# Neighbourhood attention and MLP on one core: K's window copies move from GpSimd to ScalarE, two instruction lists are reordered, and the GELU is evaluated twice

## What is computed

```python
def _na2d(x, qkv_w, qkv_b, proj_w, proj_b, num_heads=8, k=3):
    qkv = x @ qkv_w + qkv_b
    q, kk, v = jnp.split(qkv, 3, axis=-1)          # q is scaled by hd ** -0.5
    nb_k = kk[:, ri, ci]                           # the 3 x 3 neighbours of each point
    nb_v = v[:, ri, ci]
    attn = softmax(einsum('bijnd,bijmnd->bijnm', q, nb_k))
    return einsum('bijnm,bijmnd->bijnd', attn, nb_v) @ proj_w + proj_b
h1 = n1_w * arcsinh(h) + n1_b
h = h + _na2d(h1, qkv_w, qkv_b, proj_w, proj_b)
h2 = n2_w * arcsinh(h) + n2_b
out = h + gelu(h2 @ mlp_w1 + mlp_b1, approximate=False) @ mlp_w2 + mlp_b2
```

## Time and profile before

| | |
|---|---|
| device time, median of 3 runs | 4930.54 us (4923.46 to 4935.97) |
| the profiled execution | 4926.99 us, its span 4925.2 us |
| busy share of the span | PE 90%, POOL 82%, DVE 76%, ACT 68% |
| granted TensorE clock, mean | 0.979 |

### The profile page before, as it was taken

One profiled execution on the slowest core, in us unless ns is written; L12 is line 12 of the kernel. 1 busy time (PEld: TensorE's weight loads), 2 busy tenths in 40 slices (PEclk: granted clock), 3 DMA queues, 4 the chain that ended last, 5 costly groups with the idle time before them and its releaser, 6 DMA issues.

```text
span 4925.2 us, 149526 instructions
## 1 busy us (share of the span) xinstructions
PE 4412.7 (90%) x53320; PEld 3254.9 (66%) x53320; DVE 3742.0 (76%) x7717; ACT 3338.3 (68%) x4865; POOL 4059.1 (82%) x5498
## 2 busy tenths in 40 slices
PE   3899999999999999999999999999999999999997
PEld 2666666666666666667666666666676666666665
DVE  4777777777778777778777777777787777787774
ACT  2676667666667666767766676666676666776774
POOL 1788888888888888888888888888888888888885
PEclk8999999999999999999999999999999999999999
DMA  3555555555555555555555555555555555555552
GB/s 79 130 129 124 126 127 128 127 129 123 125 129 131 125 125 131 126 127 133 126 123 126 127 129 127 127 124 125 128 130 125 124 128 124 129 131 125 127 125 59
DMA packets 1330837, 610.98 MB, mean 124 GB/s; under 512 B 862990, under 2 KB 1326992, under 8 KB 1327632
## 3 DMA queue, kind: packets, MB, share of 16 engines
q1 hardware_dynamic: 1330192, 601.81, 51.7%
HBM read 208.17 MB, written 135.40 MB: 70 GB/s over the span
## 4 chain that ended last, share of the span: by engine, by line
POOL 47%; issue 32%; PE 16%; ACT 3%; POOLq 1%; DVE 1%; SPq 0%; ACTq 0%; DMA 0%; DVEq 0%
PE ps L387 15%; POOL p_lo L1058 9%; POOL b_lo L1077 8%; POOL g_lo L1087 7%; POOL g_hi L1085 6%; POOL k_win L1105 5%; POOL gate L1052 5%; POOL b_hi L1075 3%; POOL k_win L1115 2%; ACT p_hi L994 1%; POOL k_win L1124 1%; ACT L1003 1%; ACT prob L993 0%; POOLq L1055 0%; POOL a_lo L1067 0%
## 5 line engine op out<-in xcount | busy, mean ns | idle before, releaser
L1058 POOL TENSOR_TENSOR p_lo<-prob,p_hi 100x512 f16<-100x512 f32 x1024 | 1341.8, 1325 | 283.4 <-ACT p_hi L994 283.4
L993 ACT ACTIVATE prob<-ps 100x512 f32<-100x512 f32 x1024 | 614.0, 600 | 968.5 <-PE ps L387 967.4
L821 DVE TENSOR_REDUCE ps<-ps 128x8 f32<-128x800 f32 x512 | 511.0, 998 | 380.2 <-PE ps L387 377.2
L1052 POOL TENSOR_TENSOR gate<-gate_in 1x1 f32<-1x1 f32 x894 | 301.5, 337 | 488.1 <-DVE ln_u L747 434.0
L852 DVE TENSOR_TENSOR o_norm<-ps,recip 64x128 f32<-64x128 f32 x2048 | 591.3, 289 | 52.1
L1087 POOL TENSOR_TENSOR g_lo<-g,g_hi 128x512 f16<-128x512 f32 x512 | 593.2, 1159 | 40.9
L994 ACT ACTIVATE p_hi<-ps 100x512 f16<-100x512 f32 x1024 | 615.4, 601 | 0.0
L387 PEld LDWEIGHTS ps<-v_win,p_hi 100*128 100x128 f16 x8192 | 484.0, 98 | 180.1 <-issue 14.3
L387 PE MATMUL ps<-w_hi,g_hi 128*128 128x256 f16 x2048 | 559.4, 273 | 0.0
L387 PE MATMUL ps<-w_lo,g_hi 128*128 128x256 f16 x2048 | 559.4, 273 | 0.0
L387 PE MATMUL ps<-w_hi,g_lo 128*128 128x256 f16 x2048 | 559.3, 273 | 0.0
(11 more groups left out here) (105 smaller groups left out, 12676.4 us busy)
## 6 DMA issues: line engine op xcount, KB each, us to landing
keys<-k_win SPq DMA_DIRECT2D x1536, 100.0 KB, 2.2
v_win<-v_rows SPq DMA_DIRECT2D x1024, 101.6 KB
queries<-q_nat SPq DMA_DIRECT2D x1536, 64.0 KB
v_rows<-v_nat SPq DMA_DIRECT2D x256, 260.0 KB, 4.4
xin<-in_x_dram SPq DMA_DIRECT2D x128, 512.0 KB, 4.0
out_dram<-y SPq DMA_DIRECT2D x256, 256.0 KB, 2.7
queries<-in_query_mask_dram SPq DMA_DIRECT2D x128, 240.0 KB
keys<-in_mlp_w_dram SPq DMA_DIRECT2D x2, 512.0 KB, 6.7
```

The source lines that it names most:

```text
L821: v.tensor_reduce(maxima_of_pair(), ps[:, B_S:B_S + 2, 0:PAIRS * NK].rearrange("p n (a k) -> p n a k", k=NK), AX.X, ALU.max).then_inc(max3 ...
L993: act.activation(prob[b][0:NK], ps[0:NK, B_ST + b, :], ACT.Exp, scale=INV * INV).then_inc(prob_ready, 1)
L1052: pool.tensor_tensor(gate[:, n:n + 1], gate_in[:], gate_in[:], ALU.add)
L1058: pool.tensor_tensor(p_lo[b][0:NK], prob[b][0:NK], p_hi[b][0:NK], ALU.subtract).then_inc(p_lo_ready, 1)
```

## The change

K's window copies become ScalarE instructions: the 4 copies of 640 numbers stay four, the 8 copies of 80 become 2 of 320. They stand in slot 0 (bottom rows and high parts) and at the end of slot 2 (low parts and top rows). The GELU is evaluated twice on ScalarE, to fp32 and to fp16, and GpSimd's four casts go. Five of GpSimd's seven `pass_waits` go with the groups that they stood in. On ScalarE the second `q_high` moves next to the first, and `log1_` moves from behind the two tiles of slot 3 to ahead of them. On VectorE the second `q_low` moves up to the first, `sign1` moves up ahead of tile 6's normalisation, and `magnitude1` and `magnitude2` move down.

```diff
@@ VectorE, step
-                    if k == 1 and post:
-                        magnitude2(t - 1, old)
                     if k == 1 and pre:
                         q_low(t + 2, par, 0)
-                    if k == 2 and fill:
-                        magnitude1(t + 3, (u + 3) % XT)
+                        q_low(t + 2, par, 1)
+                    if k == 1 and fill:
+                        x_from_transposes(t + 3, (u + 3) % XT, 0)
...
+                    if k == 3 and fill:
+                        sign1(t + 3, (u + 3) % XT)
 
                     if att:
                         sum_reciprocal(t, 2 * k)
...
                     if k == 1 and post:
+                        magnitude2(t - 1, old)
                         sum2_(t - 1)
...
+                    if k == 2 and fill:
+                        magnitude1(t + 3, (u + 3) % XT)
                     if k == 2 and fin:
                         result(t - 2, 0)
@@ ScalarE
+            def windows_main(t, par, lo):
+
+                act.wait_ge(k_lo_ready, signals(t, G, G))
+                act.wait_ge(k_in[par], landed(t - 2, K_DMAS))
+                for g in range(G):
+                    a = k_nat[:, lo, g]
+                    rows = bass.AP(a.tensor, a.offset, [list(a.ap[0]), [TS, TILES], [PITCH, TS], [1, WIN]])
+                    to = k_win[par][:, lo, g].rearrange("p c (r j) -> p c r j", j=WIN)
+                    s = act.activation(to[:, :, 1:1 + TS], rows, ACT.Copy)
...
+            def windows_top(t, par):
+
+                act.wait_ge(k_in[par], landed(t - 2, K_DMAS))
+                window_edge(par, 0, TS - 1).then_inc(win_top, 1)
...
-                    act.activation(g32[:, m, :], ps[:, IN_BANK[m], :], ACT.Gelu, bias=b1[:, m:m + 1],
+                    act.activation(g32[:, m, :], ps[:, IN_BANK[m], :], ACT.Gelu, bias=b1[:, m:m + 1], scale=INV)
+                    act.activation(g_hi[:, m, :], ps[:, IN_BANK[m], :], ACT.Gelu, bias=b1[:, m:m + 1],
                                    scale=INV).then_inc(gelu_ready, 1)
@@ ScalarE, step
+                    if k == 3 and fill:
+                        log1_(t + 3)
                     if att:
                         probabilities(t, 2 * k)
@@ GpSimd
-                    pool.tensor_copy(g_hi[:, m, :], g32[:, m, :]).then_inc(g_hi_ready, 1)
-                    pool.wait_ge(g_hi_ready, signals(t, MT, m + 1))
```

More of the change, by code:

```diff
@@ L142, in build @@
         b2 = sb("b2", [P, C], F32)
-        gate_in, gate = sb("gate_in", [1, 1], F32), sb("gate", [1, 7], F32)
+        gate_in, gate = sb("gate_in", [1, 1], F32), sb("gate", [1, 2], F32)
         xin = sb("xin", [P, BLOCKS, C], F32)
@@ L215, in build @@
             sem("act_" + s) for s in ("q_hi", "k_hi", "v_hi", "o_hi", "gelu", "prob", "p_hi"))
-        a_hi_ready, a_lo_ready, b_hi_ready, b_lo_ready, g_hi_ready, g_lo_ready, p_lo_ready = (
-            sem("pool_" + s) for s in ("a_hi", "a_lo", "b_hi", "b_lo", "g_hi", "g_lo", "p_lo"))
-        win_main, win_bottom, win_top = (sem("pool_win_" + s) for s in ("main", "bottom", "top"))
+        a_hi_ready, a_lo_ready, b_hi_ready, b_lo_ready, g_lo_ready, p_lo_ready = (
+            sem("pool_" + s) for s in ("a_hi", "a_lo", "b_hi", "b_lo", "g_lo", "p_lo"))
+        win_main, win_bottom, win_top = (sem("act_win_" + s) for s in ("main", "bottom", "top"))
         block = ctx.enter_context(nc.Block())
@@ L892, in step @@
                         h_from_projection(t - 1, old, (u - 1) % XT, 1)
-                    if k == 1 and pre:
-                        q_low(t + 2, par, 1)
                     if k == 1 and fill:
-                        x_from_transposes(t + 3, (u + 3) % XT, 0)
                         x_from_transposes(t + 3, (u + 3) % XT, 1)
                     if k == 1 and post:
+                        magnitude2(t - 1, old)
                         sum2_(t - 1)
@@ L907, in step @@
                         result(t - 2, 1)
-                    if k == 3 and fill:
-                        sign1(t + 3, (u + 3) % XT)
                     if att:
@@ L972, in k_high, with window_edge, windows_bottom @@
                                ACT.Identity, bias=bqk[:, G + g:G + g + 1]).then_inc(k_hi_ready, 1)
+            def windows_main(t, par, lo):
[6 more added lines that the diff above has]
+                    s = act.activation(to[:, :, 1:1 + TS], rows, ACT.Copy)
+                if lo == 1:
+                    s.then_inc(win_main, 1)
+            def window_edge(par, at, row):
+                a = k_nat[:, 0, 0]
+                rows = bass.AP(a.tensor, a.offset + row * PITCH,
+                               [list(a.ap[0]), [TS * PITCH, 2 * G], [TS, TILES], [1, WIN]])
+                to = k_win[par][:].rearrange("p l g c (r j) -> p (l g) c r j", j=WIN)
+                return act.activation(to[:, :, :, at], rows, ACT.Copy)
+            def windows_bottom(t, par):
+                act.wait_ge(k_lo_ready, signals(t + 1, G, G))
+                window_edge(par, WIN - 1, 0).then_inc(win_bottom, 1)
+            def windows_top(t, par):
+                act.wait_ge(k_in[par], landed(t - 2, K_DMAS))
+                window_edge(par, 0, TS - 1).then_inc(win_top, 1)
             def v_high(t, n):
@@ L1021, in step @@
                         k_high(t + 2, 1)
+                    if k == 0 and pre and has(t + 1):
+                        windows_bottom(t + 1, old)
+                    if k == 0 and pre:
+                        windows_main(t + 2, par, 0)
                     if k == 1 and pre:
                         q_high(t + 2, par, 0)
+                        q_high(t + 2, par, 1)
                     if k == 1 and post:
                         square2(t - 1, old)
-                    if k == 1 and pre:
-                        q_high(t + 2, par, 1)
-                    if k == 1 and post:
                         log_of_square(ln2_s[:], sq2, ln2a, t - 1)
@@ L1037, in step @@
                         root(ln1_s[:], ln1a, root1, t + 3)
-                    if k == 3 and fill:
-                        log1_(t + 3)
+                    if k == 2 and pre:
+                        windows_main(t + 2, par, 1)
+                    if k == 2 and pre and fill:
+                        windows_top(t + 3, old)
                     if k == 3 and post:
@@ L1087, in g_parts @@
                     pool.tensor_tensor(g_lo[:, m, :], g32[:, m, :], g_hi[:, m, :], ALU.subtract).then_inc(g_lo_ready, 1)
[L1089 to L1125, removed]
@@ L1127, in step @@
             def step(t, u):
-                par, old = u % 2, 1 - u % 2
-                att, pre, post, fin, fill = has(t), has(t + 2), has(t - 1), has(t - 2), has(t + 3)
+                att, post, fin, fill = has(t), has(t - 1), has(t - 2), has(t + 3)
                 for k in range(SLOTS):
@@ L1132, in step @@
                         p_low(t, 2 * k)
-                    if k == 2 and pre:
-                        windows_main(t + 2, par, 1)
                     if att:
@@ L1138, in step @@
                         g_parts(t - 2, (0, 1))
-                    if k == 0 and pre and has(t + 1):
-                        windows_bottom(t + 1, old)
                     if k == 1 and fin:
                         g_parts(t - 2, (2, 3))
-                    if k == 1 and pre:
-                        windows_main(t + 2, par, 0)
                     if k == 2 and post:
@@ L1148, in step @@
                         a_parts(t + 3)
-                    if k == 3 and pre and fill:
-                        windows_top(t + 3, old)
             run(pool, step)
```

6 lines of the change are left out of this document (3 added, 3 removed).

## The result

The changed kernel takes **5100.66 us** (median of 4 runs, 5094.26 to 5103.87) against 4930.75: a ratio of 1.035, 95% interval 1.0331 to 1.0369. Slower was forecast, but 4995 and at most 5080.

A forecast was written before the change was run, and what follows sets the result against it. GpSimd's queue with a hop over TensorE and VectorE was taken as the bound, to be replaced by a 36.82 us ring. 128 x (36.82 - 36.16) = 84, less 18, on 4926.99 plus 3.5 gave 4996, stated 4995; range 4820 to 5080.

The forecast's parts named there:

- the ring: Predicted chain per band over TensorE, VectorE to `sum1_`, then ScalarE from `log1_` to the next tile 0: period 36.82 us.
- Steps 1, 2 and 4: Tile 0 to `q_product`'s end, 10.52 us; VectorE in slot 1, next maximum at 18.37; ScalarE's `log1_` to next tile 0, 10.84.
- P0: Start of tile 0's exponentials in a band, time 0 of the prediction's count.
- "So 6.3" of step 3: VectorE in slot 2: about 4.65 us without collisions, plus 0.8 at `sign2` and 0.85 at `magnitude1`; `log1_` starts at 25.98.
- the prediction's own formula: Whole kernel's time for any band period P: 4912 + 128 x (P - 36.16) us.
- fewer collisions: VectorE in slot 2: `sign2` goes ahead of GpSimd's `p_lo`, period 35.2 to 36.2, time 4790 to 4915 us; chance 0.25.
- The row or the rule: ScalarE: GELUs 0.577 us apart by trace, 0.614 by the skill; strided copies penalised by the skill without a price.
- The loop's end: Last band of each pass: 4.9 of its 5.54 us excess stays, so 0.6 x 30 passes = 18 us gained.

The follow-up runs named there:

- the third: The changed kernel with K's window copies back on GpSimd, GELU twice and new lists kept: 4914.49 us, ratio 0.9971 to the kernel before.
- the seventh experiment: The changed kernel with `magnitude1` moved to slot 1 on VectorE, behind `sum2_`: 4815.9 us, ratio 0.9766 to the kernel before.
- The fourth: The changed kernel with `sum1_` one place earlier on VectorE, ahead of `result` 0: 4923.94 us, ratio 0.9991 to the kernel before.
- The sixth: The changed kernel with `log1_` back behind tiles 6 and 7 on ScalarE: 4904.36 us, ratio 0.9946 to the kernel before.

## Why the prediction was right and wrong

**Right: the ring, and nearly each of its numbers.** Steps 1, 2 and 4 were met: second `q_low` at 11.43 after P0 (11.57 forecast), next maximum at 18.40 (18.37), `sign2` at 19.71 (19.68), `log1_` to P0 10.86 (10.84). GpSimd was busy for 21.97 (under 26) and ScalarE for 31.40 (about 32). The copies were hidden, with 0.72 and 0.47 a little longer than the 0.6 to 0.7 and 0.3 to 0.4 forecast. TensorE waited 0.92 for the second GELU (1.4).

**Wrong: the term "So 6.3" of step 3.** It measured 7.16 (19.71 to 26.87). The collisions of `sign2` and `magnitude1` were there, 0.5 and 0.9 long against 0.8 and 0.85. The third, of `sum1_` with the second `b_lo`, was put at nothing, and no reason was given. `sum1_` asked 0.09 us after `b_lo` had begun and waited 0.93 us per band, or 119 us over 128 bands; in all 25 bands between 2000 and 3000 us of the span it took 2.1. Without it the step is 6.23, close to 6.3, partly by luck: a wait 0.3 shorter than forecast makes up for small gaps in the list. By the prediction's own formula a period of 37.73 gives 4912 + 201 = 5113, against 5101 measured.

That such waits lengthen the band is shown by the third and the seventh experiment. VectorE's list is as long there as in the changed kernel, and what `sign2`, `magnitude1` and `sum1_` are shorter by (1.55 and 2.06 us) comes back in the period (1.55 and 2.19). The fourth took 177 us back by one place, about half of it as wait and half as list. The sixth adds what the prediction didn't look at: with `log1_` behind the tiles `sum1_` waits as long, but off the ring. It is `log1_`'s new place that makes VectorE's waits count.

**The range was wrong for the same reason.** The rival "fewer collisions" had the port's waits going one way only, down. A sum whose terms are ties has the same step upwards, and the third tie was not priced: with 119 us on top of 4995 the range would have reached 5114 and held the result.

**The row or the rule.** The GELUs of the changed kernel follow each other by 0.57 (the first at 2546.96, the eighth and last at 2550.96). By the figures of the Trainium skill, "ScalarE: Activation LUTs", section "What ACT_TABLE_LOAD costs", it would be 0.614, an estimate; the trace doesn't agree, and the row decided rightly. A copy of 640 numbers in rows of ten took 0.72 on ScalarE, between 0.60 for 512 and 1.06 for 1024. The Trainium skill, "SBUF — State Buffer", section "SBUF: two separate sides", has a penalty for each crossing into a new 16-byte line; these runs show none. In every collision above one of VectorE and GpSimd waited until about the end of the other's instruction: `sum1_` asked at 2539.97, `b_lo` ended at 2541.04, and `sum1_` ended 1.08 behind that, where it takes 1.22 when it waits for nothing. The same section of the Trainium skill calls their shared port pair an exclusive lock, which whoever starts first keeps for its whole instruction; these rows agree.

**The loop's end.** Forecast were 4.9 us over an inner band. Between 400 and 4600 us of the span, the last bands of 27 passes of the changed kernel took 41.25 to 43.59, mean 42.32: 4.6 over 37.73. Those of 28 passes of the kernel before took 38.79 to 41.97, mean 41.14: 5.0 over 36.16. So the 41.70 of the earlier trace rows was longer than the mean, and 0.4 us per pass were gained and not 0.6. What makes these bands vary stays open.

**What the parts are worth.** Window copies alone -0.95%; the second GELU alone +1.45% (76 us), and 120 to 178 us in the three pairs with the new lists that differ by it alone. In the changed kernel `log1_` ahead of the tiles costs 196 us and `sum1_` behind `result` 0 177. These two overlap and can't be added: with `log1_` behind the tiles `sum1_`'s wait is off the ring. Copies and GELU together with the new lists gave +3.5%, and the new lists as they stand are a part of the loss.

## What to carry to other kernels

When an engine is relieved, follow the next ring through all lists with the trace's durations: here its steps came out within 0.15 us, where no collision was in them. But where VectorE's and GpSimd's SBUF instructions meet, look for ties: 0.1 us in who starts first decided 0.9 us per band here, it can fall either way, and both ways belong in the range. Put VectorE's long instructions between SBUF tiles where GpSimd is idle. If an instruction has to wait, put it behind those of its list that could already run. And don't add work to an engine behind such a wait.

## What the runs showed of the hardware

- Less work on GpSimd made VectorE slower, and more made it faster: with K's copies on GpSimd the band was 36.18 us long, with them on ScalarE, where they hid in its waits, 37.73. Three durations on VectorE, set by who came first, make up the 1.55 us. With another order the same move cost 430 us.
- `sum1_`, asked for 0.6 us earlier, ended no earlier (24.68 and 24.70 us from P0 to `log1_`): 1.52 us long at the one place, 2.13 at the other, where it came 0.11 us behind the start of a GpSimd instruction.
- ScalarE copies rows of ten fp16 numbers at about the price of any other 640: 722 ns, where 512 took 0.60 and 1024 1.06 us, which makes 0.72 for 640 (an estimate by a straight line). GpSimd took 833 for them, waits included.
